# Longer passes, a longer lag and a mask added by VectorE in a fused attention and feed-forward kernel on eight cores

## The chip, the cores and the metric

The kernel runs on the 8 cores of one Trainium2 chip (trn2). Each core takes two of the 16 sequences and there is no traffic between cores. The metric is the time on the device in microseconds of the slowest core. Cores 0 to 3 are one die, cores 4 to 7 the other.

## The reference

```python
xn = layernorm(x)                                  # x: 16 x 2048 x 1024, f32
Q, K, V = xn @ Wq, xn @ Wk, xn @ Wv                # 1024 -> 128
logits = Q K^T / sqrt(128), -inf above the diagonal
attn_out = softmax(logits) @ V @ Wo                # 128 -> 1024
hidden = xn @ W1 + b1                              # 1024 -> 4096
q = hidden + (cos(th)*wr + sin(th)*wi) * wi * sin(th + 0.1*hidden) * 0.1
out = x + attn_out + relu(q) @ W2 + b2             # 4096 -> 1024
```

## The kernel before

**Groups and units.** A core works on 16 groups of 256 tokens (two tiles of 128 tokens each; a sequence is eight groups). The feed-forward part is cut into units: one unit is one group and one chunk of 128 of the 4096 hidden features. `f1` (line 497) is the first matmul of a unit, eight matmuls of 256 columns (line 506) into one of two PSUM banks `psW`. ScalarE takes the sine (line 514), VectorE combines it with the bank (line 519, which frees the bank: the next but one `f1` waits for it), and `relu` of the unit before (line 526) writes the 256 results to one of `NRB` = 12 buffers `rb`. That ReLU is done by VectorE (line 536), and for even units from 4 up to `RELU_ACT` = 16 by ScalarE (line 532). `f2` (line 574) is the second matmul, four matmuls of 512 columns (line 587), one into each of four PSUM banks `psO` that hold the 256 x 1024 sums.

**Units, passes and lag.** For the first two groups the units alternate between group 0 and group 1, because the weights are still coming in and each piece then serves twice. The `psO` banks hold the sums of one group alone, so the second matmuls of these two groups go in passes (line 472): group 0 chunks 0 to 5, group 1 chunks 0 to 5, group 0 chunks 6 to 11, and so on, five passes for each group. At the end of a pass `evict` (line 541) adds the four banks into the residual tiles `X` by four VectorE additions (line 545). The first `f2` of the next pass waits, bank by bank, for these (line 584). From group 2 on a group is one pass. The last three `f2` of a pass are issued as one batch, bank by bank; the batch waits at its start for the ReLU of all its three units and for all their pieces of W2 (lines 579 and 580).

**Order.** The program is written as slots: slot n issues `f1(n)`, then what `plan` holds for that slot, then `f2` turns as long as the slot is at least `lag` ahead of the turn (lines 807 to 821). The lag is 9 up to slot 61 and then `LAG` = 5; it is two less at two slots after the start of each tile's exponential and one less at the next two (lines 673 and 674). Every engine executes its instructions in the order in which they are issued there. For the first six tiles of attention (J = 0 to 5) `plan_tile` gives the slots (lines 788 to 793), for the later groups `plan_att`.

**Attention.** `logits` (line 384) makes up to four pieces of 512 columns. In the last piece a second matmul (line 396) of an identity with the mask adds -1e9 above the diagonal. VectorE copies each piece to `lg` and takes its maximum in the same instruction (line 401), then one small reduction gives the row's maximum (line 407). `expo` (line 410) loads the table of the exponential (line 412), computes it with the sum (line 414) and loads the table of the sine again (line 417), all on ScalarE; VectorE makes the reciprocal (line 419). For J below 6 VectorE scales an identity (line 426) and the probabilities are transposed by matmuls with it (`probs_t`, line 442) and copied by ScalarE (line 450). From J = 6 on VectorE scales the probabilities (line 422) and a DMA transposes them (`probs_move`, line 429).

**LayerNorm.** `ln_stats` (line 279): statistics by VectorE (lines 283, 284 and 286), then GpSimd adds the epsilon (line 288) and takes the power of -0.5 (line 291); `ln_norm` (line 298) by VectorE; the tiles 0 to 7 are transposed by TensorE (line 309) and copied by ScalarE or VectorE (lines 321 and 322). Tile 6 has its statistics in slot 44 and its norm in slot 45, tile 4 in slots 21 and 22, tile 5 in slots 30 and 31.

**Weights.** W1 and W2 are loaded once, by GpSimd's queue, converted from f32 to bf16 on the way, in 26 pieces each: 20 pieces of one chunk (256 KB in bf16) and 6 of two. The calls of `load_w1` (line 191) and `load_w2` (line 198) from line 729 to line 761 are the order of the queue. All tiles of x, the results and the transposes by DMA go through SyncE's queue.

Of the kernel before, what the change touches and what calls it, by code (L numbers as in the profile page):

```python
# [91 lines left out]
def build_nc():  # L92
# [17 lines left out]
    with ExitStack() as ctx:  # L110
# [168 lines left out]
        def ln_stats(tile, buf):  # L279
# [7 lines left out]
            pool.after(t)  # L287
            t = pool.mark(lambda e: e.tensor_scalar(  # L288
# [95 lines left out]
        def logits(J, si):  # L384
            g, half = divmod(J, 2)
            w = seg_w(J, si)
            last = si == n_seg(J) - 1
            b, free = take_bank()
            pe.after(t_q[g], t_k[g], t_mask, t_idn, free)
            fn = lambda e: e.matmul(  # L390
                psA[b][:, 0:w], Q_fm[:, half * 128:(half + 1) * 128],
                K_fm[:, si * 512:si * 512 + w], start=True, stop=not last,
                skip_group_check=True)
            if last:
                pe.do(fn)
# [3 lines left out]
            t = pe.mark(fn)
            dve.after(t, state["exp"])  # L400
            t = dve.mark(lambda e: e.tensor_scalar(  # L401
                lg[:, si * 512:si * 512 + w], psA[b][:, 0:w], 1.0, None,
                ALU.mult, ALU.max, accum_out=mx[:, si:si + 1]))
            bank_free[b] = t
            if last:
                dve.after(t)
                t_max[J] = dve.mark(lambda e: e.tensor_reduce(
                    mx[:, 4:5], mx[:, 0:si + 1], AX.X, ALU.max, negate=True))

        def expo(J):  # L410
# [4 lines left out]
                pr[:, 0:n], lg[:, 0:n], AF.Exp, bias=mx[:, 4:5],  # L415
# [4 lines left out]
            if J >= 2 * (XBAR - 1):  # L420
# [51 lines left out]
        passes = [(g, a, b) for a, b in ((0, 6), (6, 12), (12, 18), (18, 25), (25, 32))  # L472
# [17 lines left out]
        rb_free = [(i, None) for i in range(NRB)]  # L490
# [170 lines left out]
        def usual_lag(slot):  # L661
            return 9 if slot < 62 else LAG
# [236 lines left out]
```

How the kernel before makes its waits and increments, by code:

```python
    def after(self, *tokens):  # L56
        for tok in tokens:
            if tok is None:
                continue
            sem, value = tok
            if self.passed.get(sem.name, 0) >= value:
                continue
            self.passed[sem.name] = value
            self.items.append(lambda e, sem=sem, value=value: e.wait_ge(sem, value))
# [4 lines left out]
    def mark(self, fn):  # L69
        self.count += 1
        self.items.append(lambda e: fn(e).then_inc(self.sem, 1))
        return (self.sem, self.count)
# [13 lines left out]
    def start(self, queue, fn):  # L86
        self.n += 16
        queue.do(lambda e: fn(e).then_inc(self.sem, 16))
        return (self.sem, self.n)
```

## Time and profile before

| | us |
|---|---|
| median of 3 runs (lowest, highest) | 1017.58 (1016.54, 1018.67) |
| the profiled execution's own time | 1017.47 |
| its span, slowest core (7) | 1015.7 |
| spans of cores 0 to 7 | 1014.8, 1012.8, 1014.2, 1013.8, 1013.1, 1013.8, 1015.3, 1015.7 |
| busy in the span: matmuls (PE) | 1000.2 (98%) |
| weight loads (PEld) | 688.7 (68%) |
| VectorE (DVE) | 600.8 (59%) |
| ScalarE (ACT) | 396.6 (39%) |
| GpSimd (POOL) | 86.8 (9%) |

A profile is of one execution; its rows below are of core 7, the slowest, unless a core is named. Times in a timeline count from the start of the span. PE is TensorE. Matmuls are pipelined: each begins before the one in front has ended, so their shown durations overlap and a busy share of 98% holds short waits too. What a matmul costs the engine is the distance from its start to the start of the next.

### The profile page before, as it was taken

Reading aid. Unit: us, or ns where it says so; the run is one execution under the profiler, and the core shown is the slowest. Engines: PE = TensorE matmul, PEld = TensorE weight load, DVE = VectorE, ACT = ScalarE, POOL = GpSimd, SP = SyncE. Lnnn points to the kernel's source line nnn. Section 1 sums busy time; section 2 is a strip of 40 time slices with the busy share of each in tenths; the row PEclk is TensorE's granted clock in tenths of the full one; section 3 lists DMA queues with packets and bytes.
Section 4 is the critical chain, followed back from the end, with each engine's and each line's share of the span. In section 5 each row is a group of like instructions: output and inputs, shape, how many; then the busy total and the mean of one; then the engine's idle time right before and its main releaser. Section 6 shows DMA issues by size and latency. Waiting matters only on the chain.

```text
span 1015.7 us, 21157 instructions; the slowest of 8 cores (1012.8 to 1015.7 us)
## 1 busy us (share of the span) xinstructions
PE 1000.2 (98%) x7387; PEld 688.7 (68%) x7387; DVE 600.8 (59%) x1512; ACT 396.6 (39%) x741; POOL 86.8 (9%) x154
## 2 busy tenths in 40 slices
PE   8999999999999999999999999999999999999998
PEld 7666567676666766667676666766667676676665
DVE  4666766656566665565555555656566656655544
ACT  3355433433444344442433444344443434444321
POOL 5700110100001000010100001000010100000000
PEclk9999999999999999999999999999999999999999
DMA  9999952644335453453523325343453633514421
GB/s 183 174 177 177 180 113 64 124 84 79 73 78 114 89 111 54 85 117 86 113 67 69 80 72 113 82 103 66 92 89 72 129 83 76 91 43 103 97 50 43
DMA packets 89080, 98.85 MB, mean 97 GB/s; under 512 B 61968, under 2 KB 62096, under 8 KB 88976
## 3 DMA queue, kind: packets, MB, share of 16 engines
q1 hardware_dynamic: 76448, 62.87, 26.2%
q0 software_dynamic: 12384, 34.61, 21.1%
q8 instruction: 60, 0.98, 0.4%
q14 instruction: 44, 0.36, 0.1%
q10 hardware_dynamic: 144, 0.03, 0.0%
HBM read 84.02 MB, written 16.78 MB: 99 GB/s over the span
## 4 chain that ended last, share of the span: by engine, by line
PE 93%; DVE 3%; issue 2%; ACT 1%; DMA 1%; POOL 0%; DVEq 0%; SPq 0%; ACTq 0%; POOLq 0%
PE psW L506 42%; PE psO L587 42%; PE psA L342 3%; PE psA L459 1%; PE psA L390 1%; PE psA L362 1%; PE psO L566 1%; DVE X L545 1%; DMA X<-x 1%; DVE u L519 0%; ACT ss L514 0%; PE psO L506 0%; PE psA L309 0%; DVE bn L283 0%; ACT L417 0%
## 5 line engine op out<-in xcount | busy, mean ns | idle before, releaser
L506 PE MATMUL psW<-xn,W_sb 128*128 128x256 bf16 x4064 | 519.6, 273 | 4.8 <-DVE u L519 4.4
L587 PE MATMUL psO<-W_sb,rb 128*128 128x512 bf16 x2048 | 505.4, 379 | 1.7 <-DVE X L545 1.5
L506 PEld LDWEIGHTS psW<-xn,W_sb 128*128 128x128 bf16 x4064 | 395.0, 98 | 136.1 <-issue 8.1
L514 ACT ACTIVATE ss<-psW,ph_sb 128x256 bf16<-128x256 f32 x508 | 237.8, 474 | 566.8 <-PE psW L506 370.3
L519 DVE SCALAR_TENSOR_TENSOR u<-ss,Rp_sb,psW 128x256 f32<-128x256 bf16 x508 | 243.5, 479 | 304.2 <-ACT ss L514 303.6
L587 PEld LDWEIGHTS psO<-W_sb,rb 128*128 128x128 bf16 x2048 | 198.8, 98 | 170.0 <-issue 4.4
L536 DVE TENSOR_SCALAR rb<-u,fp_sb 128x256 bf16<-128x256 f32 x506 | 177.7, 351 | 47.7 <-DVE u L519 21.8
L545 DVE TENSOR_TENSOR X<-psO,X 128x512 f32<-128x512 f32 x96 | 59.8, 681 | 2.5 <-PE psO L587 2.5
L712 POOL DMA_DIRECT2D X<-b2rep x32 | 29.6, 925 | 310.8 <-DMA X<-x 295.7
L288 POOL TENSOR_SCALAR rs<-mv 128x1 f32<-128x1 f32 x32 | 7.9, 246 | 560.0 <-DVE mv L286 516.9
L401 DVE TENSOR_SCALAR_CACHE_REDUCE lg<-psA 128x512 f32<-128x512 f32 (+2 forms) x80 | 48.3, 603 | 0.0
L412 ACT ACT_TABLE_LOAD x32 | 41.1, 1283 | 0.6
L417 ACT ACT_TABLE_LOAD x32 | 41.1, 1283 | 0.6
L414 ACT ACTIVATE pr<-lg,mx 128x128 bf16<-128x128 f32 (+15 forms) x32 | 38.5, 1202 | 0.4
L342 PE MATMUL psA<-xn,Wqkv_sb 128*128 128x256 bf16 x256 | 30.6, 273 | 0.0
L390 PE MATMUL psA<-K_fm,Q_fm 128*128 128x512 bf16 (+2 forms) x80 | 27.8, 347 | 0.0
L342 PEld LDWEIGHTS psA<-xn,Wqkv_sb 128*128 128x128 bf16 x256 | 25.0, 98 | 2.9
L419 DVE RECIPROCAL sm<-sm 128x1 f32<-128x1 f32 x32 | 5.2, 162 | 33.0 <-ACT pr L414 32.8
L298 DVE TENSOR_SCALAR xn_tm<-X,mv,rs 128x1024 bf16<-128x1024 f32 x29 | 23.4, 807 | 1.3 <-POOL rs L291 1.2
L283 DVE BATCH_NORM_STATS2 bn<-X 128x6 f32<-128x512 f32 x32 | 22.0, 686 | 3.7 <-DMA X<-x 3.7
L284 DVE BATCH_NORM_STATS2 bn<-X 128x6 f32<-128x512 f32 x32 | 21.6, 675 | 0.0
L459 PE MATMUL psA<-pT,V_tm 128*128 128x128 bf16 x272 | 20.4, 219 | 0.0
(60 smaller groups left out, 281.6 us busy)
## 6 DMA issues: line engine op xcount, KB each, us to landing
X<-x SPq DMA_DIRECT2D x60, 512.0 KB, 6.3
X<-b2rep POOLq DMA_DIRECT2D x32, 512.0 KB, 6.3
out<-X SPq DMA_DIRECT2D x64, 256.0 KB, 3.0
W_sb<-w POOLq DMA_DIRECT2D x40, 256.0 KB, 25.6
W_sb<-w POOLq DMA_DIRECT2D x12, 512.0 KB, 68.6
Wqkv_sb<-wqkv POOLq DMA_DIRECT2D x1, 768.0 KB, 19.8
pT<-pr SPq DMA_TRANSPOSE x26, 3.7
xn<-xn_tm SPq DMA_TRANSPOSE x24, 3.3
```

What stands on the lines that cost most here:

```text
L342: fn = lambda e, k=k, col=col, w=w: e.matmul(psA[b][:, col:col + GT], w[:, k * DK:(k + 1) * DK], xg[:, k * GT:(k + 1) * GT], start=(k == 0 ...
L390: fn = lambda e: e.matmul(psA[b][:, 0:w], Q_fm[:, half * 128:(half + 1) * 128], K_fm[:, si * 512:si * 512 + w], start=True, stop=not last, ...
L401: t = dve.mark(lambda e: e.tensor_scalar(lg[:, si * 512:si * 512 + w], psA[b][:, 0:w], 1.0, None, ALU.mult, ALU.max, accum_out=mx[:, si:si ...
L412: act.do(lambda e: e.preload_act_table_set("exp_and_others"))
L414: state["exp"] = t_exp[J] = act.mark(lambda e: e.activation(pr[:, 0:n], lg[:, 0:n], AF.Exp, bias=mx[:, 4:5], accum_out=sm[J % 2][:, 0:1]))
L417: act.do(lambda e: e.preload_act_table_set("trig_and_small"))
L506: fn = lambda e, k=k: e.matmul(bank[:, 0:GT], w1_block(c, k), xg[:, k * GT:(k + 1) * GT], start=(k == 0), stop=(k == NCD - 1), skip_group_ ...
L514: t_sin[u] = act.mark(lambda e: e.activation(sines, bank[:, 0:GT], AF.Sin, scale=0.1, bias=ph_sb[:, c:c + 1]))
L519: t_stt[u] = dve.mark(lambda e: e.scalar_tensor_tensor(u2[u % 2][:], sines, Rp_sb[:, c:c + 1], bank[:, 0:GT], ALU.mult, ALU.add))
L536: t_relu[u] = dve.mark(lambda e: e.tensor_scalar(rb_of[u][:], u2[u % 2][:], b1c[:, c:c + 1], 0.0, ALU.add, ALU.max))
L545: partial[g, i] = bank_out[i] = dve.mark(lambda e: e.tensor_tensor(xt[:, h * 512:(h + 1) * 512], psO[i][:], xt[:, h * 512:(h + 1) * 512], ...
L587: fn = lambda e, i=i, tt=tt, h=h, u=u, c=c: e.matmul(psO[i][:], rb_of[u][:, tt * 128:(tt + 1) * 128], W2_sb[:, c * D + h * 512:c * D + (h ...
```

## The change

The first two groups take four passes each instead of five (chunks 0 to 5, 6 to 13, 14 to 22, 23 to 31), and up to slot 61 a second matmul follows eleven units behind its slot instead of nine. For that there are four more `rb` buffers, in the second half of `pT`, for the units below 64. The ReLU of the even units from 4 to 62 is ScalarE's. The mask is added by VectorE: one addition of 128 columns and one reduction of them, while the fused copy leaves these 128 columns out. Tile 5 has its probabilities transposed by a DMA, issued one slot after its exponential. The epsilon is added by VectorE. At the start `phases` comes ahead of the statistics of tile 0, VectorE copies tile 3's transposes, and six idle matmuls go. The pieces of the weights are loaded in another order.

```diff
-RELU_ACT = 16
+XBAR_TILE = 5
+RELU_ACT = 64
...
-            pool.after(t)
-            t = pool.mark(lambda e: e.tensor_scalar(
+            dve.after(t)
+            t = dve.mark(lambda e: e.tensor_scalar(
                 rs[i][:, 0:1], mv[i][:, 1:2], LNEPS, None, ALU.add))
...
-            pe.after(t_q[g], t_k[g], t_mask, t_idn, free)
-            fn = lambda e: e.matmul(
+            pe.after(t_q[g], t_k[g], free)
+            t = pe.mark(lambda e: e.matmul(
                 psA[b][:, 0:w], Q_fm[:, half * 128:(half + 1) * 128],
-                K_fm[:, si * 512:si * 512 + w], start=True, stop=not last,
-                skip_group_check=True)
+                K_fm[:, si * 512:si * 512 + w], start=True, stop=True,
+                skip_group_check=True))
+            dve.after(t, state["exp"])
+            seen = w - 128 if last else w
+            if seen:
+                t = dve.mark(lambda e: e.tensor_scalar(
+                    lg[:, si * 512:si * 512 + seen], psA[b][:, 0:seen], 1.0, None,
+                    ALU.mult, ALU.max, accum_out=mx[:, si:si + 1]))
             if last:
-                pe.do(fn)
-                fn = lambda e: e.matmul(
-                    psA[b][:, w - 128:w], idn_sb[:], mask_sb[:], start=False,
-                    stop=True, skip_group_check=True)
...
+                own = lg[:, si * 512 + seen:si * 512 + w]
+                top = si + 1 if seen else si
+                dve.after(t_mask)
+                t = dve.mark(lambda e: e.tensor_tensor(
+                    own, psA[b][:, seen:w], mask_sb[:], ALU.add))
+                dve.after(t)
+                t = dve.mark(lambda e: e.tensor_reduce(
+                    mx[:, top:top + 1], own, AX.X, ALU.max))
                 dve.after(t)
                 t_max[J] = dve.mark(lambda e: e.tensor_reduce(
-                    mx[:, 4:5], mx[:, 0:si + 1], AX.X, ALU.max, negate=True))
+                    mx[:, 5:6], mx[:, 0:top + 1], AX.X, ALU.max, negate=True))
+            bank_free[b] = t
...
-            if J >= 2 * (XBAR - 1):
+            if J >= XBAR_TILE:
...
-        passes = [(g, a, b) for a, b in ((0, 6), (6, 12), (12, 18), (18, 25), (25, 32))
+        passes = [(g, a, b) for a, b in ((0, 6), (6, 14), (14, 23), (23, 32))
...
+        rb_all = [r[:] for r in rb] + [pT[:, T // 2 + i * GT:T // 2 + (i + 1) * GT]
+                                       for i in range(4)]
+        rb_free = [(i, None) for i in range(len(rb_all))]
...
+            if u >= 64:
+                rb_free[:] = [f for f in rb_free if f[0] < NRB]
...
-            return 9 if slot < 62 else LAG
+            return 11 if slot < 62 else LAG
...
-                at(t0 + 2 * (si // 2), lambda si=si: probs_t(J, si))
+                if J < XBAR_TILE:
+                    at(t0 + 2 * (si // 2), lambda si=si: probs_t(J, si))
             at(e0, lambda: expo(J))
+            if J >= XBAR_TILE:
+                at(e0 + 1, lambda: probs_move(J))
...
+        t_rp, t_ph = phases(t_sc)
         stats(0)
         load_w1(4)
-        t_rp, t_ph = phases(t_sc)
...
-        load_all((2, 0), (2, 1), (2, 2), (2, 3), (2, 4), (2, 5), (1, 7), (1, 8), (1, 9),
+        load_all((2, 0), (2, 1), (1, 7), (2, 2), (2, 3), (2, 4), (2, 5), (1, 8), (1, 9),
                  (1, 10))
         t_wqkv = l_wqkv.start(pool, lambda e: e.dma_start(Wqkv_sb[:], wqkv))
-        load_all((1, 11), (2, 6), (2, 7), (1, 12), (2, 8), (2, 9), (2, 10), (2, 11),
-                 (1, 13), (1, 14))
+        load_all((1, 11), (1, 12), (2, 6), (2, 7), (1, 13), (2, 8), (2, 9), (1, 14))
         t_wo = l_wo.start(pool, lambda e: e.dma_start(Wo_sb[:], wo))
-        load_all((1, 15), (1, 16), (1, 17), (2, 12), (2, 13), (1, 18), (2, 14), (2, 15),
-                 (2, 16), (2, 17), (1, 19), (1, 20), (1, 21), (2, 18), (2, 19), (1, 22),
-                 (2, 20), (2, 21), (2, 22), (1, 23), (1, 24), (1, 25), (2, 23), (2, 24),
-                 (2, 25))
+        load_all((2, 10), (2, 11), (2, 12), (2, 13), (1, 15), (1, 16), (1, 17), (1, 18),
+                 (1, 19), (1, 20), (2, 14), (2, 15), (2, 16), (2, 17), (1, 21), (2, 18),
+                 (2, 19), (2, 20), (2, 21), (1, 22), (1, 23), (1, 24), (2, 22), (1, 25),
+                 (2, 23), (2, 24), (2, 25))
...
-        for tile in (2, 3):
-            at(1, lambda tile=tile: ln_transpose(tile, *tms[tile], norms[tile], act))
-            at(1, lambda: idle_work(16))
+        at(1, lambda: ln_transpose(2, *tms[2], norms[2], act))
+        at(1, lambda: idle_work(16))
+        at(1, lambda: ln_transpose(3, *tms[3], norms[3], dve))
+        at(1, lambda: idle_work(10))
...
-        for g, p in ((0, 6), (1, 7)):
+        for g, p in ((0, 4), (1, 5)):
             after_turn[turn_of[p] + 2] = [lambda g=g: wo_share(g)]
```

## Rows read from the trace of the kernel before

**Rows 1.** Groups by shape: line engine op tiles shapes xcount | busy us, mean ns | idle before.
```profile
L506 PE MATMUL psW<-xn,W_sb 128*128 128x256 bf16 x4064 | 519.6, 273 | 4.8 <-DVE u L519 4.4 <-ACT xn L321 0.2
L587 PE MATMUL psO<-W_sb,rb 128*128 128x512 bf16 x2048 | 505.4, 379 | 1.7 <-DVE X L545 1.5 <-issue 0.2
...
L536 DVE TENSOR_SCALAR rb<-u,fp_sb 128x256 bf16<-128x256 f32 x506 | 177.7, 351 | 47.7 <-DVE u L519 21.8 <-PE psW L506 1.9 <-PE psO L587 1.1
...
L396 PE MATMUL psA<-mask_sb,idn_sb 128*128 128x128 bf16 x32 | 7.0, 219 | 0.0
...
L414 ACT ACTIVATE pr<-lg,mx 128x2048 bf16<-128x2048 f32 x2 | 4.0, 2002 | 0.0
...
L532 ACT ACTIVATE rb<-u,fp_sb 128x256 bf16<-128x256 f32 x6 | 3.0, 498 | 0.0
...
L401 DVE TENSOR_SCALAR_CACHE_REDUCE lg<-psA 128x128 f32<-128x128 f32 x8 | 2.3, 282 | 0.0
```


**Rows 2.** Timeline, 58 to 75 us: start us, us, engine line op tiles xcount [idle before, releaser].
```profile
60.55 2.75 PE L587 MATMUL psO<-W_sb,rb 128*128 128x512 bf16 x12
...
64.16 2.48 DVE L545 TENSOR_TENSOR X<-psO,X 128x512 f32<-128x512 f32 x4
...
65.00 0.38 PE L587 MATMUL psO<-W_sb,rb 128*128 128x512 bf16 x1 [0.38 <-DVE X L545]
...
66.79 0.38 PE L587 MATMUL psO<-W_sb,rb 128*128 128x512 bf16 x1 [0.22 <-DVE X L545]
...
68.74 1.04 PE L506 MATMUL psW<-xn,W_sb 128*128 128x256 bf16 x8
```


**Rows 3.** Waits of PE from 150 to 950 us: us in total, times, longest.
```profile
PE psO L587 <- DVE X L545: 0.2, 1, 0.2
```


**Rows 4.** Stretches of core 7: window and length, busy us (instructions) by engine, clock, DMA share, GB/s.
```profile
11.00:13.00 2.00, 0.00 (x0) 0.00 (x0) 1.74 (x4) 0.00 (x0) 1.15 (x2) 1.00 1.06 157
...
15.00:17.00 2.00, 1.82 (x18) 1.52 (x16) 1.90 (x5) 1.01 (x1) 0.83 (x3) 0.50 0.99 163
17.00:19.00 2.00, 2.00 (x18) 1.58 (x17) 1.15 (x3) 0.29 (x1) 1.31 (x3) 0.67 1.10 164
...
64.00:66.00 2.00, 1.37 (x12) 0.63 (x10) 1.94 (x5) 0.47 (x1) 0.00 (x0) 1.00 1.04 227
```


**Rows 5.** One issue of a W1 piece (line 196), core 7: start, us to landing.
```profile
L196 POOL DMA_DIRECT2D W_sb<-w x1: 805/805/805, 31.5 to 31.5; - x1
...
DMA to landing us min/median/max: 37.0/37.0/37.0
```


**Rows 6.** Timeline, 98 to 121 us.
```profile
106.76 1.03 PE L506 MATMUL psW<-xn,W_sb 128*128 128x256 bf16 x8 [1.19 <-DVE u L519]
...
108.60 1.28 ACT L412 ACT_TABLE_LOAD   x1
...
110.92 0.16 DVE L419 RECIPROCAL sm<-sm 128x1 f32<-128x1 f32 x1 [1.91 <-ACT pr L414]
...
112.70 0.48 DVE L519 SCALAR_TENSOR_TENSOR u<-ss,Rp_sb,psW 128x256 f32<-128x256 bf16 x1 [0.93 <-ACT ss L514]
...
115.44 1.03 PE L506 MATMUL psW<-xn,W_sb 128*128 128x256 bf16 x8
115.90 0.81 DVE L298 TENSOR_SCALAR xn_tm<-X,mv,rs 128x1024 bf16<-128x1024 f32 x1 [0.60 <-POOL rs L291]
...
117.51 1.03 PE L506 MATMUL psW<-xn,W_sb 128*128 128x256 bf16 x8 [0.75 <-DVE u L519]
```


**Rows 7.** The same piece's issue on core 6.
```profile
L196 POOL DMA_DIRECT2D W_sb<-w x1: 710/710/710, 32.2 to 32.2; - x1
...
DMA to landing us min/median/max: 38.3/38.3/38.3
```


**Rows 8.** Timeline, 128.5 to 139 us.
```profile
128.63 1.04 PE L506 MATMUL psW<-xn,W_sb 128*128 128x256 bf16 x8
...
132.73 0.16 DVE L419 RECIPROCAL sm<-sm 128x1 f32<-128x1 f32 x1 [1.86 <-ACT pr L414]
```

More of the change, by code:

```diff
@@ L388, in logits @@
             b, free = take_bank()
-            pe.after(t_q[g], t_k[g], t_mask, t_idn, free)
-            fn = lambda e: e.matmul(
+            pe.after(t_q[g], t_k[g], free)
+            t = pe.mark(lambda e: e.matmul(
                 psA[b][:, 0:w], Q_fm[:, half * 128:(half + 1) * 128],
-                K_fm[:, si * 512:si * 512 + w], start=True, stop=not last,
-                skip_group_check=True)
-            if last:
-                pe.do(fn)
-                fn = lambda e: e.matmul(
-                    psA[b][:, w - 128:w], idn_sb[:], mask_sb[:], start=False,
-                    stop=True, skip_group_check=True)
[L399 to L405, printed above, removed]
+                K_fm[:, si * 512:si * 512 + w], start=True, stop=True,
[6 more added lines that the diff above has]
+                    ALU.mult, ALU.max, accum_out=mx[:, si:si + 1]))
+            if last:
+                own = lg[:, si * 512 + seen:si * 512 + w]
[6 more added lines that the diff above has]
+                    mx[:, top:top + 1], own, AX.X, ALU.max))
                 dve.after(t)
                 t_max[J] = dve.mark(lambda e: e.tensor_reduce(
-                    mx[:, 4:5], mx[:, 0:si + 1], AX.X, ALU.max, negate=True))
+                    mx[:, 5:6], mx[:, 0:top + 1], AX.X, ALU.max, negate=True))
+            bank_free[b] = t
         def expo(J):
@@ L414, in expo @@
             state["exp"] = t_exp[J] = act.mark(lambda e: e.activation(
-                pr[:, 0:n], lg[:, 0:n], AF.Exp, bias=mx[:, 4:5],
+                pr[:, 0:n], lg[:, 0:n], AF.Exp, bias=mx[:, 5:6],
                 accum_out=sm[J % 2][:, 0:1]))
@@ L489, in build_nc @@
             lg[:, 1536 + 128 * i:1664 + 128 * i].bitcast(BF16) for i in range(NWIDE - 2)]
-        rb_free = [(i, None) for i in range(NRB)]
+        rb_all = [r[:] for r in rb] + [pT[:, T // 2 + i * GT:T // 2 + (i + 1) * GT]
+                                       for i in range(4)]
+        rb_free = [(i, None) for i in range(len(rb_all))]
         rb_of, rb_ix = {}, {}
@@ L527, in relu @@
             c = units[u][1]
+            if u >= 64:
+                rb_free[:] = [f for f in rb_free if f[0] < NRB]
             i, free = rb_free.pop(0)
-            rb_of[u] = rb[i]
+            rb_of[u] = rb_all[i]
             if on_act(u):
@@ L532, in relu @@
                 t_relu[u] = act.mark(lambda e: e.activation(
-                    rb_of[u][:], u2[u % 2][:], AF.Relu, bias=b1c[:, c:c + 1]))
+                    rb_of[u], u2[u % 2][:], AF.Relu, bias=b1c[:, c:c + 1]))
             else:
@@ L536, in relu @@
                 t_relu[u] = dve.mark(lambda e: e.tensor_scalar(
-                    rb_of[u][:], u2[u % 2][:], b1c[:, c:c + 1], 0.0,
+                    rb_of[u], u2[u % 2][:], b1c[:, c:c + 1], 0.0,
                     ALU.add, ALU.max))
@@ L776, in build_nc @@
         res[0], res[1] = [0, 1], [2, 3]
-        turn_of = {p: sum(b - a for _, a, b in passes[:p]) for p in range(11)}
-        for g, p in ((0, 6), (1, 7)):
+        turn_of = {p: sum(b - a for _, a, b in passes[:p]) for p in range(9)}
+        for g, p in ((0, 4), (1, 5)):
             after_turn[turn_of[p] + 2] = [lambda g=g: wo_share(g)]
```

## The prediction

> **What bounds the kernel now.** I read the shares of the engines first, then the groups by shape, then the timeline of the first 150 us, and last the issues of the weights. TensorE is the bound: 4064 matmuls of 256 columns and 2048 of 512 fill the span [rows 1], and no other engine passes 59%. But the shown busy time hides waits: four second matmuls start at 65.00 to 66.79 us, 0.60 us apart, each waiting for VectorE to empty its bank [rows 2], where they run 0.216 us apart otherwise ((2.75 - 0.38) / 11 of the batch at 60.55 [rows 2]). A first matmul of 256 columns takes 0.110 us ((1.04 - 0.272) / 7 [rows 1, 2]), so `f1` of a unit costs 0.87 us, `f2` 0.86 us, a batch 2.6 us. Counting so, from start to start, TensorE waits some 6 us between 68.7 and 150 us, and next to nothing from 150 to 950 us [rows 3]. The first 150 us are also those in which the weights come in: the DMA share is 1.04 at 64 to 66 us [rows 4], a full queue.
>
> **Work removed from TensorE.** The 32 mask matmuls go [rows 1], 128 columns each. By the two sizes above 128 columns cost about 0.056 us; 30 of them lie behind 69 us: 1.7 us. Tile 5's six transposing matmuls are 0.3 us. Together **-2.0 us**. A mask matmul is not hidden, since TensorE is the bound, so this comes back whole.
>
> **The start.** Five small VectorE operations leave the way of tile 1's statistics, GpSimd's addition goes to VectorE, tile 3 is copied by VectorE, six idle matmuls go. I put this at 1.2 us earlier (between 0 and 2). It does not enter the sum, because of the next step.
>
> **The second pass and its weights.** The slots, written out by hand from the diff, give group 0's pass of chunks 6 to 13 its batch (chunks 11, 12, 13) in slot 26. It waits for piece 13 of W2. In the new order this piece is the 24th of the second stretch of the queue, with the same bytes ahead of it as piece 16 of W1 has now. That one was issued at 31.5 us and landed 37.0 us later, at 68.5 us [rows 5]. The queue is full, so the place in it sets the time: W2 piece 13 lands at **68.5 us**, within 1 us.
>
> When would TensorE be there? Before, `f1(27)` starts at 68.7 [rows 2], with 20 second matmuls done. The new order has 17 done at that point: 68.7 - 2.6 = 66.1. The four bank waits (1.7 us) are not there, since `f1` and attention stand between this eviction and the next pass; the start gives 1.2; against that come 0.6 us at units 9 to 11, which have no `f2` between them (a bank is free some 2.4 us after its `f1` began: the matmuls, a sine and a combination of 0.48 us each [rows 6] and three hand-overs, against 1.74 for two `f1`), and 1.0 us in slots 22 to 25, where four evictions, the statistics and norm of tile 4 and the new mask operations queue on VectorE. That is 66.1 - 1.7 - 1.2 + 1.6 = 64.8 us. So TensorE stands idle for about 3.7 us, and `f1(27)` starts at 68.5 + 2.6 = 71.1 instead of 68.7: **+2.4 us**, with all the gain of the start swallowed. On core 6 the same place of the queue lands at 32.2 + 38.3 = 70.5 us [rows 7], so the slowest core may be worse off by up to 2 us.
>
> **The clock.** An idle TensorE may lose its clock. From 11 to 13 us it did nothing on core 7, and from 15 to 17 us the granted clock is 0.50, the level of 1.2 GHz, though it had worked in between; from 17 to 19 us the mean is 0.67 [rows 4]. That is 3.3 us at half rate (2.0, and 0.33 / 0.5 of the next two), with what is beside it 1.7 us of full-rate work. The wait at 65 us would be longer than that idle time. Bounds: 0 and 1.7; the nearest row is the one just named, so I take **+1.7 us**. The Trainium skill says the same (TensorE: Matmul & The Clock Gate, "Loop structure matters more than you think"): a long DMA wait between matmuls lets the array run cold. By this rule the term stands; if the clock holds, the sum is 1.7 less.
>
> **Evictions behind LayerNorm, slots 43 to 46.** The new pass 14 to 22 ends in slot 45. VectorE's order there is: reciprocal of tile 4 (waits for the exponential), `relu(43)`, slot 44's combination, statistics of tile 6, slot 45's combination, norm of tile 6, and only then the four evictions. Take the start of `f1(43)` as zero (106.76 before [rows 6]). The exponential's table load starts at +1.84, the reciprocal at +4.16, slot 44's combination at +5.94, the norm ends at +9.95 [rows 6]. `relu(42)` now stands ahead of the exponential on ScalarE, 0.50 us [rows 1], and the combination no longer waits behind `relu(44)`. So the norm ends at about +10.3 and the banks are free at +11.0 and then every 0.62 us (2.48 / 4 [rows 2]). On TensorE the batch cannot start before `relu(43)`, at about +5.5, where it would arrive at +3.7; it ends at +8.1, `f1(46)` at +9.0, and `f2` of the next pass stands in slot 46 itself: it starts at +11.0 and ends at +13.1. Its work alone takes 8.0, so 5.1 us of waiting; before, `f1(47)` starts at 115.44, +8.7, so 0.6. **+4.5 us** (bounds: 0, if the evictions come ahead of the norm in effect, and 5).
>
> **Slot 54.** The pass 14 to 22 of group 1 ends in the slot of tile 5's exponential. The reciprocal starts 4.1 us behind `f1(54)` [rows 8], the scaling of 768 probabilities follows (I take 0.4 us; the ReLU of 256 f32 values is 0.35 [rows 1]), then the evictions, with the banks free from +5.7 to +7.5. `f2` of the next pass arrives at +5.2 and ends at +7.8 instead of +6.1: 1.7 us, where the old pass end in slot 56 costs 0.5. **+1.2 us**.
>
> **Waits that go.** The one of 1.3 us ahead of `f1(43)` [rows 6] comes from the eviction of slot 40, which is no more. The one ahead of `f1(48)`, 117.51 [rows 6], is 0.9 us by starts and is met while VectorE is already late. Slots 50 to 53 have an `f2` each now, 0.6 us. **-2.8 us**. Against that, slots 27 to 34, where the exponential of tile 1 and tile 5's statistics now follow a batch, cost some 0.5 us more.
>
> **VectorE and ScalarE elsewhere.** The mask costs VectorE an addition and a reduction (0.28 us each by the nearest row, the fused copy of 128 columns [rows 1]), less what the shorter copy saves: some 0.45 us for each tile. The exponential of 2048 columns has no idle time before it, nor have the 15 other sizes [rows 1]: they wait for the table load and not for the maximum, which hides the longer chain. What is left is a delay of the combination behind the mask. TensorE's waits for VectorE are 0.2 us in 800 [rows 3]; how much room lies under that no grouped view says. I take 0, with 3.3 us (half of the 26 tiles by 0.25) as the upper end. ReLUs on ScalarE: 24 of 0.50 us against 0.35 on VectorE [rows 1], in a stretch where both have room: 0. The transfer of tile 5's probabilities stands in SyncE's queue behind nothing that is late; the next things in the queue are the stores of slot 62: 0.
>
> **The sum.** 2.4 + 1.7 - 2.0 + 4.5 + 1.2 - 2.8 + 0.5 = +5.5 us, on the profiled execution's 1017.5 (span 1015.7 and 1.8 around it; the median of the runs is 1017.6): **1023.0 us**.
>
> **The rivals.**
> - *The wait for W2 is there, the late evictions are not.* If VectorE gets through its queue in slots 43 to 54 as it does now, the +4.5 and +1.2 and the -2.8 and +0.5 cancel to about 0: 1017.5 + 2.4 + 1.7 - 2.0 = 1019.6, or 1017.9 with the clock held. Against it: VectorE executes in order. Chance 0.17, 0.10 of it within the bound.
> - *The weights are there in time and the evictions too: faster.* If the piece lands before 65 us, `f1(27)` starts at 67.4, 1.3 us early, the mask and the transposes give 2.0, and fewer passes cost nothing: 1014.2 us. It decides at slot 26: it needs a landing 3.7 us ahead of what the queue's place gives, or a wait that is half so long with all other waits at their old size. Chance 0.15.
> - *Weights in time, evictions late:* 1014.2 + 3.4 = 1017.6. Chance 0.06.
> - *The mask on VectorE also delays the later groups:* 1023.0 + 3.3 = 1026.3. For it: slots 17 to 21, where `f1` follow each other with few `f2` between. Against it: no wait there now [rows 3]. Chance 0.10.
> - My forecast: 0.52.
>
> What a measurement of this kernel can tell from no change is 0.2%, 2 us. **Slower** by more: 0.52 + 0.10 + 0.07 = 0.69; **same**: 0.10 + 0.06 = 0.16; **faster**: 0.15. The range leaves out the faster rival and a little above the last: from 1015.5 (the first rival with a wait shortened by 2 us) to 1026.5.
>
> **What would show it.** Right: TensorE has a gap ahead of the batch of slot 26 with a W2 piece as its releaser and a landing near 68.5 us; a dip of the clock behind it; near 115 us four L587 matmuls 0.6 us apart, behind the norm of tile 6; all matmuls from 160 us on as close as before. Wrong: a batch at 65 us without a gap (then the faster rival), or VectorE's evictions at +8 us behind `f1(43)`. The forecast falls if the weights come faster than now, or if TensorE reaches slot 26 only at 68 us.

## The result, and the profile after

| | before | after |
|---|---|---|
| median of the runs, us (number) | 1017.45 (6) | 1026.51 (6) |
| the profiled execution's own time | 1017.47 | 1026.39 |
| spans, slowest and fastest core | 1015.7, 1012.8 | 1024.8, 1021.9 |

One of the six runs of after was disturbed (1213 us) and is left out of the ratio. The changed kernel is slower: the ratio is 1.0088, 95% interval 1.0077 to 1.0099, some 9 us where the prediction had +5.5; its range ended at 1026.5, so the time lies on its upper edge. The slowest core of the profile is core 2, but 125 matmul records of it are missing, so the rows below are of core 7 (span 1023.6), whose records are complete and which was also core 7 in the rows of before (span 1015.7).

To see where the 8 us of core 7 come from I compare the starts of the same `f1(u)` in the two traces. At `f1(27)` both kernels have 20 second matmuls behind them, and from `f1(64)` on the lag is the same, so these points stand for the same work:

| core 7, us | start of `f1(27)` | `f1(27)` to `f1(64)` | `f1(64)` to the last matmul |
|---|---|---|---|
| before | 68.7 | 83.7 | 858.7 |
| after | 74.3 | 87.5 | 857.5 |
| difference | +5.6 | +3.8 | -1.2 |

Core 7 was one of two cores of before that ran at the lower clock at 15 us [rows 4], and its `f1(27)` was the latest of all (66.3 to 68.7 us). As the weights decide when `f1(27)` comes after the change (73.6 to 75.3 us), the typical core lost more than core 7: the median spans of the two dies were 1014.0 and 1014.5 us before and are 1023.5 and 1023.4.

**The wait for W2.** The issue of W2's piece 13 on core 7 (start, us to landing, who waited), where [rows 5] have what stood in that place before:

```profile
L204 POOL DMA_DIRECT2D W_sb<-w x2: 738/744/749, 29.6 to 30.1; - x2
...
  PE psO L599: 4.7, 1
...
DMA to landing us min/median/max: 38.0/38.5/39.0
```

The second of these two issues lands at 30.1 + 39.0 = 69.1 us. The timeline around it shows who stood there, as in [rows 2]:

```profile
63.51 1.04 PE L516 MATMUL psW<-xn,W_sb 128*128 128x256 bf16 x8
...
69.24 5.24 PE L599 MATMUL psO<-W_sb,rb 128*128 128x512 bf16 x12 [4.69 <-DMA W_sb<-w]
...
74.31 1.04 PE L516 MATMUL psW<-xn,W_sb 128*128 128x256 bf16 x8
```

TensorE is through with `f1(26)` at 63.51 + 0.87 = 64.4 us and stands idle for 4.9 us. Then the same twelve matmuls that took 2.6 us before take 74.31 - 69.24 = 5.1 us. The stretches tell why (columns as in [rows 4], the clock third from the end): the clock fell while TensorE was idle and came back only behind the batch. They also show a second fall of the clock that nobody waited for:

```profile
66.00:68.00 2.00, 0.00 (x0) 0.00 (x0) 0.00 (x0) 0.00 (x0) 0.00 (x0) 0.87 1.07 181
68.00:70.00 2.00, 0.76 (x2) 0.28 (x3) 0.00 (x0) 0.00 (x0) 0.00 (x0) 0.50 1.09 185
70.00:72.00 2.00, 2.00 (x6) 0.73 (x5) 0.69 (x1) 0.00 (x0) 0.00 (x0) 0.50 1.11 185
72.00:74.00 2.00, 2.00 (x6) 0.70 (x5) 1.35 (x2) 0.00 (x0) 0.00 (x0) 0.50 1.09 175
...
120.00:122.00 2.00, 0.88 (x3) 0.29 (x3) 2.00 (x4) 0.00 (x0) 0.31 (x1) 1.00 1.02 168
122.00:125.50 3.50, 3.30 (x17) 2.26 (x17) 0.97 (x3) 0.58 (x2) 1.53 (x2) 0.51 1.03 191
```

**The late evictions.** The timeline of core 7 from `f1(43)` to `f1(47)`, which stands for [rows 6]:

```profile
109.73 1.04 PE L516 MATMUL psW<-xn,W_sb 128*128 128x256 bf16 x8
...
114.28 0.16 DVE L426 RECIPROCAL sm<-sm 128x1 f32<-128x1 f32 x1 [1.88 <-ACT pr L421]
...
115.39 2.75 PE L599 MATMUL psO<-W_sb,rb 128*128 128x512 bf16 x12 [1.42 <-DVE rb L548]
...
116.47 0.69 DVE L284 BATCH_NORM_STATS2 bn<-X 128x6 f32<-128x512 f32 x1
...
119.12 0.81 DVE L299 TENSOR_SCALAR xn_tm<-X,mv,rs 128x1024 bf16<-128x1024 f32 x1 [0.37 <-POOL rs L292]
119.85 2.48 DVE L557 TENSOR_TENSOR X<-psO,X 128x512 f32<-128x512 f32 x4
...
120.68 0.38 PE L599 MATMUL psO<-W_sb,pT 128*128 128x512 bf16 x1 [1.67 <-DVE X L557]
...
122.85 1.91 PE L516 MATMUL psW<-xn,W_sb 128*128 128x256 bf16 x8
```

The batch ends near 118, but VectorE is busy with the statistics and the norm of tile 6 and empties the banks from 119.85 on, so the four matmuls of the next pass start 0.6 us apart behind it. `f1(47)` then runs at half rate (1.91 us instead of 1.04). Slot 54 has the same pattern on a smaller scale (for [rows 8]):

```profile
136.55 1.04 PE L516 MATMUL psW<-xn,W_sb 128*128 128x256 bf16 x8
...
140.60 0.16 DVE L426 RECIPROCAL sm<-sm 128x1 f32<-128x1 f32 x1 [1.86 <-ACT pr L421]
140.87 0.42 DVE L429 TENSOR_SCALAR pr<-pr,sm 128x768 bf16<-128x768 bf16 x1
141.21 2.48 DVE L557 TENSOR_TENSOR X<-psO,X 128x512 f32<-128x512 f32 x4
...
143.83 0.38 PE L599 MATMUL psO<-W_sb,pT 128*128 128x512 bf16 x1 [0.22 <-DVE X L557]
```

**In sum.** The waits of PE from 25 to 165 us (us in total, times, longest), after:

```profile
PE psO L599 <- DMA W_sb<-w: 5.4, 2, 4.7
PE psO L599 <- DVE X L557: 3.2, 8, 1.7
PE psW L516 <- DVE u L529: 1.7, 4, 0.5
PE psO L599 <- DVE rb L548: 1.4, 1, 1.4
PE psA L466 <- ACT K_fm L354: 1.1, 1, 1.1
```

and in the same stretch before:

```profile
PE psW L506 <- DVE u L519: 3.9, 6, 1.2
PE psO L587 <- DVE X L545: 1.5, 6, 0.4
```

The waits for a bank of `psW` fell by 2.2 us, as the change would have it, and 5.4 us of weights, 1.7 us of evictions, 1.4 us of a ReLU and 1.1 us of a weighted sum (line 466, near `f1(30)`) came in their place. From 165 to 950 us the view of waits has no row at all for PE, where [rows 3] had one of 0.2 us. The groups by shape that answer to [rows 1]:

```profile
L516 PE MATMUL psW<-xn,W_sb 128*128 128x256 bf16 x4064 | 519.7, 273 | 2.9 <-DVE u L529 2.2 <-ACT xn L322 0.7
L599 PE MATMUL psO<-W_sb,rb 128*128 128x512 bf16 x1992 | 495.8, 380 | 7.1 <-DMA W_sb<-w 5.4 <-DVE rb L548 1.4 <-DVE X L557 0.2
...
L410 DVE TENSOR_REDUCE mx<-lg 128x1 f32<-128x128 f32 x32 | 9.1, 286 | 3.6
L407 DVE TENSOR_TENSOR lg<-psA,mask_sb 128x128 f32<-128x128 f32 x32 | 9.1, 285 | 0.0
```

### The profile page after: what moved, and what is told of

It is laid out like the page before. It is cut to its first block, busy times and chain, and to the rows that moved or that the text cites. A ratio compares the mean times of both kernels' runs of the same rounds, so it can differ in the third digit from the quotient of the medians.

```text
span 1024.8 us, 21012 instructions; the slowest of 8 cores (1021.9 to 1024.8 us)
## 1 busy us (share of the span) xinstructions
PE 995.4 (97%) x7218; PEld 687.5 (67%) x7343; DVE 605.6 (59%) x1561; ACT 404.1 (39%) x762; POOL 77.2 (8%) x122
## 3 DMA queue, kind: packets, MB, share of 16 engines
q1 hardware_dynamic: 77248, 63.06, 21.8%
## 4 chain that ended last, share of the span: by engine, by line
PE 85%; DMA 4%; ACT 3%; DVE 3%; issue 3%; POOL 1%; DVEq 0%; ACTq 0%; SPq 0%; POOLq 0%
PE psW L516 40%; PE psO L599 38%; DMA W_sb<-w 4%; PE psA L343 2%; PE psA L466 1%; PE psO L578 1%; PE psA L363 1%; PE psA L391 1%; DVE X L557 1%; ACT pr L421 1%; ACT L419 1%; POOL W_sb L204 1%; DMA X<-x 1%; DVE u L529 1%; ACT ss L524 1%
## 5 line engine op out<-in xcount | busy, mean ns | idle before, releaser
L599 PE MATMUL psO<-W_sb,rb 128*128 128x512 bf16 x1887 | 478.1, 380 | 12.5 <-DMA W_sb<-w 5.3
L599 PEld LDWEIGHTS psO<-W_sb,rb 128*128 128x128 bf16 x1992 | 194.6, 98 | 171.4 <-issue 10.9
L548 DVE TENSOR_SCALAR rb<-u,fp_sb 128x256 bf16<-128x256 f32 x476 | 167.4, 352 | 46.0 <-DVE u L529 23.2
L292 POOL TENSOR_TENSOR rs<-rs,fp_sb 128x1 f32<-128x1 f32 x32 | 19.4, 605 | 601.2 <-DVE rs L289 479.3
L557 DVE TENSOR_TENSOR X<-psO,X 128x512 f32<-128x512 f32 x88 | 55.1, 683 | 10.9 <-PE psO L599 10.8
L399 DVE TENSOR_SCALAR_CACHE_REDUCE lg<-psA 128x512 f32<-128x512 f32 (+2 forms) x72 | 42.8, 595 | 0.0
L391 PE MATMUL psA<-K_fm,Q_fm 128*128 128x512 bf16 (+3 forms) x65 | 22.1, 340 | 0.0
```

What stands on the lines that cost most here:

```text
L391: t = pe.mark(lambda e: e.matmul(psA[b][:, 0:w], Q_fm[:, half * 128:(half + 1) * 128], K_fm[:, si * 512:si * 512 + w], start=True, stop=Tr ...
L399: t = dve.mark(lambda e: e.tensor_scalar(lg[:, si * 512:si * 512 + seen], psA[b][:, 0:seen], 1.0, None, ALU.mult, ALU.max, accum_out=mx[:, ...
L548: t_relu[u] = dve.mark(lambda e: e.tensor_scalar(rb_of[u], u2[u % 2][:], b1c[:, c:c + 1], 0.0, ALU.add, ALU.max))
L557: partial[g, i] = bank_out[i] = dve.mark(lambda e: e.tensor_tensor(xt[:, h * 512:(h + 1) * 512], psO[i][:], xt[:, h * 512:(h + 1) * 512], ...
L599: fn = lambda e, i=i, tt=tt, h=h, u=u, c=c: e.matmul(psO[i][:], rb_of[u][:, tt * 128:(tt + 1) * 128], W2_sb[:, c * D + h * 512:c * D + (h ...
```

## The experiments

The theory behind the result, to be tested: **one**, W2's pieces 10 to 13 come too late and the wait lets the clock fall (5 to 6 us); **two**, the evictions of slot 45 stand behind tile 6's LayerNorm (some 3 us); **three**, the mask and the start give back what was forecast. The rival to it: these waits are only where one longer delay shows, of the mask on VectorE or the ReLUs on ScalarE, and would move elsewhere when taken away. Ratios are against the kernel before in the same session on the same chip; the changed kernel itself has 1.0088.

**W2 first.** The changed kernel, with the four pieces ahead of W1's piece 14 and of Wo.

```diff
-        load_all((1, 11), (1, 12), (2, 6), (2, 7), (1, 13), (2, 8), (2, 9), (1, 14))
+        load_all((1, 11), (1, 12), (2, 6), (2, 7), (1, 13), (2, 8), (2, 9),
+                 (2, 10), (2, 11), (2, 12), (2, 13), (1, 14))
         t_wo = l_wo.start(pool, lambda e: e.dma_start(Wo_sb[:], wo))
-        load_all((2, 10), (2, 11), (2, 12), (2, 13), (1, 15), (1, 16), (1, 17), (1, 18),
+        load_all((1, 15), (1, 16), (1, 17), (1, 18),
```

> The changed kernel with pieces 10 to 13 of W2 ahead of piece 14 of W1 and of Wo in GpSimd's queue, nothing else. Theory 1 (the batch of slot 26 waits for W2 piece 13 by its place in the full queue): two pieces of about 1.65 us fewer ahead, so it lands near 65.8 us instead of 69.1, the gap ahead of the batch falls from 4.9 to about 1.5 us and is too short for the clock to fall, so 2.6 us more come back: 5 to 6 us faster than the changed kernel, about 1021. Rival (the wait only moves: W1 piece 14 or Wo is then late, or the time is made up later anyway): within 1 us of 1026.5.

Measured: 1021.09 us, ratio 1.0045 (1.003 to 1.006). That is 5.4 us less by the medians of the two sessions, 4.4 by the ratios. Core 7:

```profile
63.52 1.04 PE L516 MATMUL psW<-xn,W_sb 128*128 128x256 bf16 x8
65.93 2.75 PE L599 MATMUL psO<-W_sb,rb 128*128 128x512 bf16 x12 [1.37 <-DMA W_sb<-w]
68.52 1.04 PE L516 MATMUL psW<-xn,W_sb 128*128 128x256 bf16 x8
```

Piece 13 lands at 65.8 us, the batch starts 3.3 us earlier and runs at full rate; `f1(27)` is at 68.5 instead of 74.3. Nothing else was moved, so part one of the theory holds, and the time did not come back elsewhere: on core 7 the rest of the run, from `f1(27)` to the last matmul, is 943.9 us against 945.0. Two things are less even than core 7 shows. On cores 0 and 1 TensorE still waited 2.4 and 2.3 us, the clock still fell, and `f1(27)` came at 70.4. And the second fall of the clock, at 121 to 124 us in the changed kernel, is gone on six of the eight cores, though the waits ahead of it stand as before (`f1(43)` to `f1(47)` takes 12.95 us on core 7).

**Idle matmuls in the gap.** The changed kernel, with 66 matmuls of the identity ahead of the batch, that fill 3.85 us. No part of the computation is left out.

```diff
+        def fill(n):
+            b = bank_no[0] % 2
+            pe.after(bank_free[b])
+            for _ in range(n):
+                pe.do(lambda e: e.matmul(psA[b][:, 0:128], idn_sb[:], idn_sb[:],
+                                         start=True, stop=True, skip_group_check=True))
+        at(26, lambda: fill(66))
```

> The changed kernel with 66 idle matmuls of 128 columns (0.056 us each, 3.7 us) in slot 26 ahead of the batch, where TensorE waits 4.9 us. Theory 1 (the idle time costs TensorE its clock, the twelve matmuls of the batch take 0.427 instead of 0.216 us each): the clock stays at 1.0 and 2.5 us come back, about 1024. Rival (the clock dips for another reason, as the power of all cores starting at once): the dip stays and the time is the same, 1026.5.

Measured: 1025.27 us (1023.42 to 1026.95), ratio 1.0085 (1.007 to 1.01): no difference from the changed kernel that these runs can tell. The timeline of PE and two stretches, core 7:

```profile
64.56 3.85 PE L807 MATMUL psA<-idn_sb 128*128 128x128 bf16 x66
69.63 2.75 PE L599 MATMUL psO<-W_sb,rb 128*128 128x512 bf16 x12 [1.22 <-DMA W_sb<-w]
72.22 1.04 PE L516 MATMUL psW<-xn,W_sb 128*128 128x256 bf16 x8
```

```profile
68.00:70.00 2.00, 0.79 (x10) 0.46 (x8) 0.00 (x0) 0.00 (x0) 0.00 (x0) 1.00 1.07 182
70.00:72.00 2.00, 2.00 (x12) 0.88 (x9) 1.46 (x3) 0.00 (x0) 0.00 (x0) 1.00 1.11 179
```

Here the clock holds, with the weights still as late: the batch takes 2.6 us, and `f1(27)` is at 72.2 instead of 74.3. So the clock's share of the start is shown, 2.5 us. A typical core has it: the median span of the eight cores is 1020.9 to 1021.5 us in the four runs, against 1023.5 to 1023.9 in the changed kernel. The total does not, because the metric is the slowest core: in the profiled execution seven cores held their clock with 0.5 to 2.2 us of idle time left between the idle matmuls and the batch, but on core 0, with 2.25 us left, it fell and `f1(27)` was at 74.7, like the changed kernel's 73.6 to 75.3. The second fall, at 121 to 124 us, was still there on five cores. The forecast of a gain in the median missed.

**Tile 6's LayerNorm later.** The changed kernel, with statistics and norm of tile 6 behind the evictions, and the load of tile 7 one slot later, behind that norm.

```diff
-                3: (12, 13, 15, 30, 20, 31, 33),
+                3: (14, 15, 16, 30, 20, 31, 33),
```

> The changed kernel with statistics, norm and next load of tile 6 two, two and one slots later (46, 47, 48), so that the four evictions of slot 45 come ahead of them on VectorE. Theory 1 (the evictions queue behind statistics and norm): the next pass starts 2.5 to 3 us earlier, about 1023.8. Rival (the batch's own wait for the ReLU behind the exponential sets it): under 0.5 us.

Measured: 1022.63 us, ratio 1.006 (1.004 to 1.008), 3.9 us less by the medians and 2.8 by the ratios. Core 7:

```profile
115.14 2.75 PE L599 MATMUL psO<-W_sb,rb 128*128 128x512 bf16 x12 [1.43 <-DVE rb L548]
...
116.65 2.48 DVE L557 TENSOR_TENSOR X<-psO,X 128x512 f32<-128x512 f32 x4
...
118.59 1.05 PE L599 MATMUL psO<-W_sb,pT 128*128 128x512 bf16 x4
...
119.83 0.69 DVE L284 BATCH_NORM_STATS2 bn<-X 128x6 f32<-128x512 f32 x1
```

Counted from `f1(43)` the evictions start 2.9 us earlier, the four second matmuls run without a gap, and `f1(43)` to `f1(47)` takes 10.0 us instead of 13.1. The batch still waits 1.43 us for the ReLU behind the exponential. From `f1(27)` to the last matmul the eight cores take 941.0 to 941.1 us, where the changed kernel has 945.0 to 945.4 on seven cores and 943.9 on core 3. That difference of 1.0 us is the second fall of the clock: core 3 is the one core without it. It is gone here on all eight cores, though nothing was done about it but to take the wait away. With the wait in place it comes on seven cores (changed kernel), five (idle matmuls) and two (W2 first), so the wait makes the fall possible, and what decides on a single core is not shown. Part two holds: 2.9 us of waiting, and 1.0 more where the clock fell.

**The mask alone.** The kernel before, with the mask added by VectorE as in the changed kernel.

```diff
-                fn = lambda e: e.matmul(
-                    psA[b][:, w - 128:w], idn_sb[:], mask_sb[:], start=False,
...
+                t = dve.mark(lambda e: e.tensor_tensor(
+                    own, psA[b][:, seen:w], mask_sb[:], ALU.add))
+                dve.after(t)
+                t = dve.mark(lambda e: e.tensor_reduce(
+                    mx[:, top:top + 1], own, AX.X, ALU.max))
```

> The kernel before with only the mask moved to VectorE (addition and reduction of 128 columns for each tile, no mask matmul). Theory 1: TensorE is the bound and loses 32 matmuls of 0.056 us: 1.8 us faster than before, 1015.7, less up to 1 us where VectorE is late in the first 150 us. Rival (0.45 us more on VectorE in each tile delays the combination, and so f1, in the later groups): no gain or up to 3 us slower.

Measured: 1017.06 us, ratio 0.9999 (0.9989 to 1.001): nothing of the 1.8 us arrives. From `f1(27)` to the last matmul there is a gain of 0.9 us on core 7. Behind `f1(64)` it is 1.5, as 26 tiles of 0.056 us give; ahead of it the kernel is 0.6 us slower in spite of four masks less, by waits for VectorE, of which I had counted up to 1 us. The waits of PE from 150 to 950 us:

```profile
PE psO L593 <- DVE X L551: 0.2, 1, 0.2
```

It is the one row of [rows 3], so the rival that the mask delays the later groups falls. That the total shows none of the 0.9 us is within its interval of 1 us.

**The start alone.** The kernel before, with `phases` first, the epsilon and tile 3 by VectorE, and six idle matmuls fewer.

```diff
-            t = pool.mark(lambda e: e.tensor_scalar(
+            t = dve.mark(lambda e: e.tensor_scalar(
                 rs[i][:, 0:1], mv[i][:, 1:2], LNEPS, None, ALU.add))
...
+        t_rp, t_ph = phases(t_sc)
         stats(0)
...
+        at(1, lambda: ln_transpose(3, *tms[3], norms[3], dve))
+        at(1, lambda: idle_work(10))
```

> The kernel before with only the changes of the start (phases ahead of the statistics of tile 0, epsilon by VectorE, tile 3 copied by VectorE, six idle matmuls fewer). Theory 1: every unit comes 1.2 us earlier and the weights' places in the queue allow it, 1016.3 (0.5 to 1.5 us faster, at the limit of what can be told). Rival (the weights take the gain back at the next piece that is late, or the clock falls at the start as on two cores before): no difference.

Measured: 1016.75 us, ratio 0.9996 (0.9987 to 1.0006). No difference: on core 7 TensorE waits 0.6 us at 59 us for a piece of W2 that nobody waited for before. A start that is earlier than its weights gives nothing, in this order too.

**ReLUs on ScalarE alone.** The kernel before, with `RELU_ACT = 64`.

```diff
-RELU_ACT = 16
+RELU_ACT = 64
```

> The kernel before with RELU_ACT 64 alone: 24 more ReLUs on ScalarE (0.50 us each), 24 fewer on VectorE (0.35). Theory 1: both have room in the first 150 us, no difference (within 1 us of before). Rival (ScalarE is late ahead of each exponential, so the exponential, the reciprocal and all behind it come 0.5 us later for each tile): 1 to 3 us slower.

Measured: 1018.67 us, ratio 1.0012 (1.0003 to 1.0021), from `f1(27)` on 0.6 us longer on every core. I had costed this at 0. It is small, but the interval leaves 0 out.

**The lag alone.** The kernel before, with a lag of eleven and the four more buffers; passes and order of the weights as before.

```diff
-            return 9 if slot < 62 else LAG
+            return 11 if slot < 62 else LAG
```

> The kernel before with the lag of eleven units and the four more buffers alone, passes and weights' order as before. Theory 1 (the loss comes from what a batch has to wait for, not from the lag): W1 piece 7 is now needed before it lands and costs about 1 us near 35 us, the batches move to slots 25, 30, 36, 43, 51 and 56, of which 43 and 51 stand near an exponential or statistics: 0 to 3 us slower than before. Rival (the lag itself is the loss, since more first matmuls in a row wait for their banks): 5 us or more slower.

Measured: 1024.33 us, ratio 1.0066 (1.0053 to 1.0078), far more than I thought. The waits of PE from 25 to 165 us, core 7, and the longest of the second row in the timeline:

```profile
PE psW L508 <- DVE u L521: 6.9, 12, 1.4
PE psW L508 <- DMA W_sb<-w: 4.4, 2, 2.6
```

```profile
36.37 1.03 PE L508 MATMUL psW<-xn,W_sb 128*128 128x256 bf16 x8 [2.64 <-DMA W_sb<-w]
```

With a longer lag more first matmuls stand early in the program: they ask for W1 sooner than the old order brings it, and for `psW` banks while VectorE has its other work. So a longer lag is no slack for TensorE; it moves the same waits to the first matmuls unless weights and slots are laid anew. The changed kernel has its own order for that, so the 6.7 us are the lag's price on the old slots; what it costs in the new kernel is not shown. Nine-chunk passes with a lag of nine can't be laid, since a batch would come ahead of its units, so that split stays open.

**Both repairs and more.** The changed kernel with W2 first and tile 6 later, and tile 5's exponential at 57 instead of 54, tile 0's weighted sum at 31 instead of 29.

```diff
-        plan_tile(0, 22, 23, 27, 29)
+        plan_tile(0, 22, 23, 27, 31)
...
-        plan_tile(5, 48, 54, 58, 62)
+        plan_tile(5, 48, 57, 58, 62)
```

> The changed kernel with four moves together: the order of the weights of a1_w2_first, the later statistics and norm of tile 6 of a3_norm_late, the exponential of tile 5 three slots later (57) so that the evictions of slot 54 don't queue behind it, and the weighted sum of tile 0 two slots later (31) so that it doesn't wait for a bank whose copy stands behind the exponential of tile 1. Theory 1 (the waits add up and each is a matter of order): 5.4 + 3.9 as measured, and 1.2 + 1.2 by the waits of the trace, so 11 to 12 us faster than the changed kernel, 1014.5 to 1016, 1 to 2 us faster than the kernel before. Rival (longer passes and ScalarE's ReLUs cost something in themselves, or each wait removed turns up at the next): 1018 or more.

Measured: 1017.97 us, ratio 1.001 (1.0001 to 1.0019): 8 us of the 9 are back, but it misses the forecast by 2. The later weighted sum is worth 0.7 us (`f1(27)` to `f1(43)` 34.7 us instead of 35.4 on core 7). But from `f1(54)` to `f1(64)`, with the same matmuls in between, core 7 takes 27.35 us, against 25.23 in the changed kernel, with two new waits, ahead of `f1(55)` and `f1(57)`:

```profile
127.73 0.69 DVE L284 BATCH_NORM_STATS2 bn<-X 128x6 f32<-128x512 f32 x1 [3.58 <-DMA X<-x]
130.17 1.91 PE L516 MATMUL psW<-xn,W_sb 128*128 128x256 bf16 x16 [1.11 <-DVE u L529]
133.80 1.03 PE L516 MATMUL psW<-xn,W_sb 128*128 128x256 bf16 x8 [1.72 <-DVE u L529]
```

The first has nothing to do with the exponential. VectorE stands 3.58 us ahead of the statistics of tile 7, whose load the later LayerNorm has put back by a slot: issued at 116.5, it lands 11.1 us later. `f1(54)` to `f1(55)` takes 4.74 us here, and 3.46 on cores 2 and 4, where VectorE waits 1.6 and 2.2 us for the load. This costs 1.3 us of the 2.1; the moved exponential costs the other 0.8 (`f1(55)` to `f1(64)` 22.6 us instead of 21.8).

**The same, tile 5's exponential back at 54.**

```diff
-        plan_tile(5, 48, 57, 58, 62)
+        plan_tile(5, 48, 54, 58, 62)
```

> c1_repair without the move of tile 5's exponential (54 again). Theory 1: in c1_repair the exponential in slot 57 blocks the sines of slots 58 and 59, where nothing but first matmuls is to be done: f1(57) to f1(64) took 19.0 us against 16.9; put back, 2 us come back, and the queue behind the exponential of slot 54 costs 1.1 again only if the clock is lost: about 1016.0, within 0.1% of the kernel before or just ahead of it. Rival (the loss lies in the four passes, wherever the exponential stands): 1018.

Measured: 1020.22 us, ratio 1.0025 (1.0016 to 1.0034), slower than the version above, in another session and on another chip; it fits neither the forecast (1016) nor its rival (1018). From `f1(27)` on it is shorter, by 2.0 us on core 7, as expected, and by 0.0 to 1.7 on the others. Statistics of tile 7 still wait 2.1 to 2.9 us for their load. But W2's piece 13 landed at 67.4 to 68.8 us where the version above had 65.0 to 67.9, six cores lost their clock ahead of the batch instead of two, and `f1(27)` came at 70.3 to 74.0 instead of 67.8 to 73.1. The queue is the same in both, so where the batch stands at the edge of its weights, as here, the total moves by some 2 us with the landing. Why the landing differs is open; session and chip changed together.

**The old passes with the rest of the change.** The changed kernel with passes, lag and order of the weights of before.

```diff
-        passes = [(g, a, b) for a, b in ((0, 6), (6, 14), (14, 23), (23, 32))
+        passes = [(g, a, b) for a, b in ((0, 6), (6, 12), (12, 18), (18, 25), (25, 32))
...
-            return 11 if slot < 62 else LAG
+            return 9 if slot < 62 else LAG
...
-        for g, p in ((0, 4), (1, 5)):
+        for g, p in ((0, 6), (1, 7)):
```

> The changed kernel with passes, lag and order of the weights put back to those of the kernel before; mask, ReLUs, tile 5's transfer, start, epsilon and the 16 buffers stay changed. Theory 1 (passes with their weights and their evictions are the whole loss): the 9 us are gone and the rest is worth what its matmuls are worth, 0 to 3 us faster than the kernel before. Rival (ReLUs on ScalarE ahead of exponentials, or the mask on VectorE, cost a part of the 9 us): 1 us or more slower than the kernel before.

Measured: 1015.95 us, ratio 0.9989 (0.9979 to 0.9998). So all of the loss lies in the three parts that are undone, taken together, and what is left is 1 us faster than before.

**The best of these.** As the last, and the ReLUs back on VectorE (`RELU_ACT = 16`).

```diff
-RELU_ACT = 64
+RELU_ACT = 16
```

> c2_old_passes with RELU_ACT 16: the kernel before with the mask and epsilon on VectorE, the changed start and tile 5's transfer. By the runs so far ScalarE's ReLUs cost 1.2 us alone and c2_old_passes is 1.1 us faster than before: 2 us faster than before, 1015.0 to 1015.5. Rival (in c2_old_passes the ReLUs pay for themselves, since VectorE also has the mask to do): 0 to 1 us faster, or slower than c2_old_passes.

Measured: 1016.33 us against 1017.31, ratio 0.9983 (0.9974 to 0.9993). It is the fastest of all against its own kernel before, by 1.7 us (0.7 to 2.6), near the 2 us that were expected, and beats both kernels; against the version above the intervals overlap, so whether the ReLUs matter there is not shown.

## Why the prediction was right, and where it was short

The sign and the mechanism were right in each of the two places that it named, and the sum was 3.5 us short. That the time still lies at the edge of the range is in part luck: the room above 1023.0 was there for a mask that delays the later groups, which it did not do, and other terms used it up. By its own steps, on core 7:

- **The wait for W2 (+2.4).** Right in kind. The landing was 69.1, forecast 68.5, from what stood in that place before. TensorE arrived at 64.4 instead of 64.8, which changes nothing, as the landing sets the time. With 0.15 us to the start of the batch the step measures 69.24 + 2.6 - 68.7 = +3.1: 0.7 short. That a gain of the start goes under in a wait for weights fits the start alone.
- **The clock (+1.7).** This is the term that was mis-sized: it measures +2.5, shown by the batch's 5.1 us and by the 2.6 us of the version with idle matmuls. I took the price from a dip that had begun to recover [rows 4]; here all of the batch ran at 0.50. The Trainium skill (TensorE: Matmul & The Clock Gate, "Loop structure matters more than you think") has it that a long wait for a DMA leaves the array running cold. The trace agrees: the clock is at 0.50 behind the wait for the DMA.
- **Evictions behind LayerNorm (+4.5).** It measures +4.4 (13.1 us from `f1(43)` to `f1(47)`, 8.7 before). Counted from `f1(43)`: batch at +5.7 (forecast +5.5), end of the norm +10.2 (+10.3), first bank +10.95 (+11.0), `f1(47)` +13.1 (+13.1). The experiment that moves tile 6 confirms the cause for 2.9 to 3.1 us of it. The rest is the batch's wait for `relu(43)` behind the exponential, 1.43 us there as here, which no run took away.
- **Slot 54 (+1.2).** The last of the four second matmuls ends at 143.83 + 0.22 - 136.55 = +7.5, forecast +7.8. With the old pass end that goes, the net is +0.9 instead of +1.2.
- **The work removed, the waits that go, slots 27 to 34.** From `f1(27)` to `f1(64)` the steps give 4.5 + 1.2 - 2.8 + 0.5 less 0.6 us of removed work, +2.8; measured +3.8, of which 1.0 is the second fall of the clock. Singly, by starts on core 3 (no second fall) less the matmuls in between at the sizes of the prediction, an estimate: slots 27 to 34 +0.5, the wait ahead of `f1(43)` -1.35, slots 47 to 53 -1.2, where the forecast had +0.5, -1.3 and -1.5. Behind `f1(64)` the change gives -1.2, where 26 masks would give -1.5 and the mask alone does. These steps hold.
- **What was not in the sum.** The second fall of the clock, 1.0 us. I had placed a dip only behind the wait for a DMA and read the evictions as four short waits; but the same view that gave me the dip at the start would have let me ask it of the 5.1 us of waiting that I had worked out for slots 43 to 46.
- **ReLUs on ScalarE (0).** On the old slots they cost 1.2 us (0.3 to 2.1); in the changed kernel their share isn't separated. The mask on VectorE (0, upper end 3.3) costs nothing in the later groups on the old slots, and loses 0.6 us of its own gain in the first 150 us.
- **The slowest of eight.** I had allowed core 6 up to 2 us more. `f1(27)` is at 73.6 to 75.3, and core 2 with 75.3 sets the time, 1.0 us behind core 7.

So 0.7 for the landing, 0.8 for the clock, 1.0 for its second fall and 1.0 for the slowest core against the one I reckoned with make up the missing 3.5 us. The mis-sized term of the prediction is thus the clock, put at +1.7 where the batch measures +2.5 and the second fall comes on top. The two main causes are shown by experiments; the landing's spread and how the lag's price divides in the changed kernel stay open.

## What to carry to other kernels

Read the weights' queue as a timetable: ask for each batch when its last piece lands, and how far that is from the batch on the latest core of all, since an edge within 2 us is paid by one of eight. At the end of an accumulation pass, look at what stands ahead of the eviction in the order of its engine, above all a LayerNorm or a reciprocal that itself waits. And where several waits come close together, price the clock behind them too: taking 2.9 us of waiting away gave back 4.0 here on the cores where the clock had fallen. When a LayerNorm is moved behind other work, look at the load that is issued behind it: here the next tile then came too late.

## What the runs showed of the hardware

- The granted clock fell to the level of 1.2 GHz at about 122 us on seven of eight cores, without one long gap ahead of it: on core 7 the longest waits of TensorE from 112 to 122 us are 1.42 and 1.67 us. It cost 1.0 us (945.0 against 943.9 us from `f1(27)` to the last matmul on the core where it did not fall). With the waits taken away it fell on none of eight.
- In a wait of 4.9 us it fell (mean 0.87 from 66 to 68 us), stayed at 0.50 for the whole batch of twelve matmuls of 512 columns, which started 0.42 us apart ((74.31 - 69.24) / 12), and was back soon after: from 74 to 76 us its mean was 0.92.
- 66 idle matmuls of 128 columns (3.85 us) kept the clock at 1.00 through the same wait on core 7, with 1.2 us of idle time left behind them, and on six more cores, with 0.5 to 2.2 us left; on core 0, with 2.25 us left, it fell.
- The landing of the same piece, in the same order of the queue, differs by 1.4 to 3.7 us between the cores of one execution (69.1 to 70.5 us in the changed kernel, 63.3 to 67.0 with W2 first), and by 2.2 us in the mean between two sessions on two chips (65.0 to 67.9 and 67.4 to 68.8 us).
- While the weights came in, the load of a tile of x took 9.0 us to land in the changed kernel and 11.1 with both repairs (core 7, issues at 120.0 and 116.5 us).
- A mask addition and a reduction of 128 columns on VectorE take 0.285 and 0.286 us, as the bound from the fused copy of that size had it [rows 1].
